# The memory stage of a two-layer decoder: one masking operation on a difference, the best one-hot by a relu on ScalarE, 1/Z on the one-hots, buffers of their own and a new order of work

## What is computed

```python
xn = (x - mu) * rsqrt(var + BN_EPS) * gamma + beta
q = (xn @ w_q.T).reshape(b, n, 2, h, kd).transpose(2, 0, 1, 3, 4)
sim = einsum('pbnhd,hkpd->pbnhk', q, keys)            # 2 sides, 8 heads, 32 keys
s, i = top_k(sim, 8)                                  # the 8 best keys of each side
all_scores = sx[..., :, None] + sy[..., None, :]      # 64 pairs a head
scores, pk = top_k(all_scores, 8)                     # the 8 best pairs
o = gelu(inputs . key_in[idx]) * softmax(scores)
return sum over heads and pairs of o * key_out[idx]   # 1024 experts of 128 features
```

## Time and profile before

| | |
|---|---|
| median of three runs | 2841.72 us |
| the profiled execution, its own time | 2846.45 us |
| its span, first to last instruction | 2844.7 us |
| TensorE busy | 2507.1 us (88%) |
| VectorE busy | 2333.9 us (82%) |
| ScalarE busy | 1834.5 us (64%) |
| GpSimd busy | 1016.5 us (36%) |
| memory stage | from about 648 to 1431 us of the span |
| granted TensorE clock, mean | 0.934 |

### The profile page before, as it was taken

One profiled execution on the slowest core, in us unless ns is written; L12 is line 12 of the kernel. 1 busy time (PEld: TensorE's weight loads), 2 busy tenths in 40 slices (PEclk: granted clock), 3 DMA queues, 4 the chain that ended last, 5 costly groups with the idle time before them and its releaser, 6 DMA issues.

```text
span 2844.7 us, 95835 instructions
## 1 busy us (share of the span) xinstructions
PE 2507.1 (88%) x35786; PEld 1949.9 (69%) x35786; DVE 2333.9 (82%) x6239; ACT 1834.5 (64%) x3307; POOL 1016.5 (36%) x1045
## 2 busy tenths in 40 slices
PE   2999982776888888888789999989979999999999
PEld 2666651555777777777756666656678888888887
DVE  6999989786799999999779999868867777777776
ACT  1777763454566666666456666658857777777776
POOL 0444430006799999999722332211121000000000
PEclk9999995885799999999899999979959999999999
DMA  5000000000000000000010000011101111111111
GB/s 169 1 0 0 0 15 0 1 0 2 2 0 0 0 0 0 0 0 0 1 60 0 0 0 0 1 34 44 41 16 48 50 56 52 56 54 50 56 52 49
DMA packets 56796, 64.67 MB, mean 23 GB/s; under 512 B 7696, under 2 KB 35088, under 8 KB 56592
## 3 DMA queue, kind: packets, MB, share of 16 engines
q1 hardware_dynamic: 56720, 63.65, 7.4%
HBM read 59.17 MB, written 4.46 MB: 22 GB/s over the span
## 4 chain that ended last, share of the span: by engine, by line
PE 81%; DVE 10%; issue 5%; DVEq 1%; ACT 1%; POOL 1%; DMA 0%; ACTq 0%; POOLq 0%; SPq 0%
PE ps L1073 9%; PE ps L894 8%; PE ps L1062 5%; PE ps L921 5%; PE ps L936 4%; PE ps L1087 4%; PE ps L1164 4%; PE ps L1166 4%; PE ps L1142 4%; PE ps L1165 4%; PE ps L1144 4%; PE ps L1143 4%; DVE work L1596 3%; PE ps L908 3%; PE ps L949 2%
## 5 line engine op out<-in xcount | busy, mean ns | idle before, releaser
L484 POOL TENSOR_TENSOR work<-work,consts_sb 128x1024 f32<-128x1024 f32 x128 | 243.6, 1903 | 563.1 <-ACT work L612 563.1
L1073 PEld LDWEIGHTS ps<-work 32*32 32x32 f32 x16384 | 244.2, 145 | 124.8 <-issue 123.0
L1073 PE MATMUL ps<-work 32*32 32x32 f32 x16384 | 250.1, 226 | 74.2 <-DVE work L1596 61.3
L732 ACT ACTIVATE ps<-work 128x128 f32<-128x128 f32 x512 | 154.6, 354 | 236.5 <-DVE work L1578 225.4
L894 PE MATMUL ps<-work 128*128 128x512 f32 x512 | 262.1, 614 | 4.3 <-issue 4.3
L1726 DVE TENSOR_TENSOR h_low<-consts_sb,h_up 128x1024 fp32r<-128x1024 f32 x128 | 158.4, 1237 | 110.9 <-ACT h_up L803 110.7
L1142 PE MATMUL ps<-a_low,w_up 128*128 128x512 f32 x512 | 202.7, 396 | 1.5 <-DVE a_low L1701 0.9
L1164 PE MATMUL ps<-h_low,d_up 128*128 128x512 f32 x512 | 199.6, 390 | 2.3 <-DVE h_low L1726 2.3
L1726 DVE TENSOR_TENSOR h_low<-small_w,h_up 128x1024 fp32r<-128x1024 f32 x128 | 158.8, 1241 | 51.6 <-ACT h_up L803 51.6
L1144 PE MATMUL ps<-a_up,w_low 128*128 128x512 f32 x512 | 199.9, 391 | 0.0
L1143 PE MATMUL ps<-a_up,w_up 128*128 128x512 f32 x512 | 199.8, 390 | 0.0
(11 more groups left out here) (260 smaller groups left out, 6703.5 us busy)
## 6 DMA issues: line engine op xcount, KB each, us to landing
gates_spread<-gate_rows SPq DMA_DIRECT2D x128, 256.0 KB, 3.1
ctxT_all<-in_ctxT SPq DMA_DIRECT2D x1, 4096.0 KB, 12.9
work<-in_ctx SPq DMA_DIRECT2D x64, 64.0 KB, 1.8
work<-in_ctxT SPq DMA_DIRECT2D x64, 64.0 KB, 1.8
out<-x_all SPq DMA_DIRECT2D x16, 256.0 KB, 3.5
big<-in_up SPq DMA_DIRECT2D x1, 2048.0 KB, 8.5
consts_sb<-in_consts SPq DMA_DIRECT2D x1, 936.0 KB
w<-in_key_inT SPq DMA_DIRECT2D x1, 512.0 KB, 3.6
```

The source lines that it names most:

```text
L1073: ins = pe.matmul(psW[rows, n // 16, :, n % 16], XT[rows, T.u, :, n], YT[rows, T.u, :, n], start=True, stop=True)
```

## The change

GpSimd no longer builds the one-hot of the best key by a subtraction and a comparison. It takes the least kept product less the four terms for all heads at once, into a buffer LESS (`below_least`), and VectorE's `chosen` becomes one instruction: is the difference at most zero, times the term. The best one-hot comes from ScalarE: relu(1 + 2^100 * difference). The factor 1/Z is put on the two one-hots (`scaled_one_hots`, ScalarE, eight instructions, from SBUF into the strided layout `sides`) in place of the four terms (into PSUM). The differences have a buffer of their own (DIFF), so that exp is one instruction of 640 elements; IN2 becomes one of three rows of a buffer `hots`; psSim and psM get PSUM banks of their own. The lists of segments are in a new order, with larger lags on ScalarE, TensorE and VectorE, and `add_memory` is split in two.

```diff
+        DIFF = carve(BEST + 2 * NS)
-        IN2 = carve(2 * NS).rearrange("p (s h k) -> p s h k", s=2, h=PH)
+        hots = carve(3 * 2 * NS).rearrange("p (r s h k) -> p s r h k", r=3, s=2, h=PH)
+        IN2 = hots[:, :, 2]
+        LESS = w8[:, 0:NEXP].rearrange("p (n h k) -> p n h k", n=4, h=PH)
+        one_hot_sides = sides.rearrange("p (k a r h) -> p a r h k", a=4, r=2, h=PH)[:, 0:4:3]
...
-        psM = bank(4, 0)
-        psSim = ps[:, 7, :]
+        psM = bank(3, 0)
+        psSim = ps[:, 2, :]
...
                 need(pool, hot_ready, T.before(1))
+                need(pool, scaled_ready, T.before(1))
                 pool.tensor_tensor(IN2, keys_of(u), second, ALU.subtract).then_inc(less_second, 1)
...
-            def ranks(T):
-                need(pool, sides_ready, T.before(1))
-                pool.tensor_tensor(one_hot[0], keys_of(u), best_of(u)[:, :, :, 0:1].to_broadcast([P, 2, PH, NKEY]), ALU.subtract)\
-                    .then_inc(less_top, 1)
-                pool.tensor_scalar(one_hot[0], one_hot[0], 0.0, None, ALU.is_ge).then_inc(top_ready, 1)
-                pool.tensor_tensor(one_hot[1], IN2, one_hot[0], ALU.subtract).then_inc(hot_ready, 1)
-            staggered(nc, pool, NT, [(0, candidates), (0, terms), (0, ranks)])
+            def second_one_hot(T):
+                pool.wait_ge(top_ready, T.now())
+                pool.tensor_tensor(IN2, IN2, hots[:, :, T.u], ALU.subtract).then_inc(hot_ready, 1)
+            def below_least(T):
+                pool.wait_ge(t8_ready, T.now())
+                pool.wait_ge(terms_ready, T.now())
+                need(pool, xy_ready, T.before(1))
+                least = T8[:, u, :, TOPK - 1:TOPK].unsqueeze(1).to_broadcast([P, 4, PH, NKEY])
+                pool.tensor_tensor(LESS, least, terms_of(u), ALU.subtract).then_inc(share_ready, 1)
+            staggered(nc, pool, NT, [(0, candidates), (0, terms), (0, second_one_hot), (0, below_least)])
...
+                act.activation(EX[:, T.u, 0:BEST + 2 * NS], DIFF[:, :], ACT.Exp).then_inc(ex_ready, 1)
+            def best_one_hot(T):
+                act.wait_ge(d_ready, T.now())
+                need(act, scaled_ready, T.before(2))
+                act.activation(hots[:, :, T.u], keys_diff, ACT.Relu, scale=FAR, bias=1.0).then_inc(top_ready, 1)
+            def scaled_one_hots(T):
+                act.wait_ge(hot_ready, T.now())
+                act.wait_ge(rz_ready, T.now())
+                need(act, sides_ready, T.before(1))
                 for h in range(PH):
-                    ins = act.activation(psSH[:, :, h, :], terms_of(u)[:, :, h, :], ACT.Copy, scale=RZ[:, u, h:h + 1])
+                    ins = act.activation(one_hot_sides[:, :, :, h, :], one_hots_of(u)[:, :, :, h, :], ACT.Copy, scale=RZ[:, u, h:h + 1])
...
-            staggered(nc, act, NT, [(0, normed), (1, shares), (0, key_exps), (1, hidden)])
+            staggered(nc, act, NT, [(0, normed), (1, key_exps), (2, scaled_one_hots), (1, best_one_hot), (2, hidden)])
...
-            staggered(nc, pe, NT, [(0, key_scores), (2, spread_heads), (1, hidden), (3, mixed), (2, turn_weights)])
+            staggered(nc, pe, NT, [(3, spread_heads), (4, mixed), (2, hidden), (3, turn_weights), (0, key_scores)])
...
-                for h in range(PH):
-                    ins = dve.scalar_tensor_tensor(out=chosen_terms[:, :, h, :], in0=terms_of(u)[:, :, h, :],
-                                                   scalar=T8[:, u, h, TOPK - 1:TOPK], in1=psSH[:, :, h, :],
-                                                   op0=ALU.is_ge, op1=ALU.mult)
+                dve.scalar_tensor_tensor(out=chosen_terms, in0=LESS.rearrange("p n h k -> p (n h) k"), scalar=0.0,
+                                         in1=terms_of(u).rearrange("p n h k -> p (n h) k"), op0=ALU.is_le, op1=ALU.mult)\
+                    .then_inc(xy_ready, 1)
...
-            staggered(nc, dve, NT, [(0, top_keys), (0, less_best), (1, chosen), (2, turn_back), (0, top_pairs), (3, add_memory),
-                                    (1, turn_sides), (0, pair_sums), (2, gated), (0, pair_shares)])
+            staggered(nc, dve, NT, [(0, top_keys), (0, less_best), (4, add_memory), (2, turn_back), (4, stats_with_memory), (1, chosen),
+                                    (0, top_pairs), (1, turn_sides), (0, pair_sums), (2, gated), (0, pair_shares)])
```

59 lines of the change are left out of this document (28 added, 31 removed).

## The result

The changed kernel takes 2853.15 us (median of 6 runs, 2848.39 to 2857.20) against 2840.84 us of the kernel before on the same chip (6 runs, 2837.49 to 2845.20). The ratio is 1.0038, with a 95% interval of 1.0026 to 1.0050: it is slower, by 0.4%. The forecast was 2824 us, 0.6% faster, with a range from 2792 to 2852. The profiled execution took 2852.48 us with a span of 2850.7, so the span grew by 6.0 us.

What follows compares the result with a forecast made beforehand. GpSimd was taken to set the pace now, and a circle of waits after the change; 53 tiles by 0.15 us is 8, plus 10 at the ends, 18 us less: 2824 us, range 2792 to 2852.

Steps and rivals of the forecast that it cites:

- chosen (12): Forecast's spread: VectorE's chosen, taken as 1.7 us, could lie between 1.2 and 2.25; 12 us more at the upper end.
- the lock's length (7): Forecast's spread: if GpSimd locks VectorE out for all of second_one_hot's 1.08 us, not 0.95, 7 us more in all.
- The tile: Memory stage loop: steps of 11.6 and 10.8 us, mean 11.2, 0.15 less than now, 8 us over 53 tiles.
- The ends: First and last tiles of the memory stage: add_memory's waits for TensorE leave their place ahead of turn_sides; 10 us gained.
- The load of the exp table ... 1.28 us, every other tile: ScalarE, before key_exps' exp: the load is exposed in the loop's first step and hidden in the second; 1.28 us.
- L1559 to be held until 0.95 after second_one_hot starts, in every tile, because both hang on one event: VectorE's first subtraction of less_best, behind the scaled copies, is locked out by GpSimd; first step 11.6 us.
- The same step for the second tile: Loop's second step: candidates held by chosen until 3.4, terms at 3.75, the same 0.95 us hold; 10.8 us.
- no change: Rival: TensorE's clock dips or queueing around chosen keep the tile at 11.3 us; 2842 us; chance 0.12.
- one of the prediction's own signs of being wrong: Prediction wrong if less_best's first subtraction is short, the copies take 3 us or more, or VectorE waits for TensorE again.
- The sizes: Instruction times taken from similar ones: second_one_hot 1.08 us and below_least 1.90 on GpSimd, chosen 1.7 on VectorE.
- Strided writes are slow on ScalarE: Rival: the eight scaled copies pay for strides, 0.86 us later; 2856 us with the lock, chance 0.16; without, 2818, 0.10.
- No lock: Rival: GpSimd and VectorE miss each other, a tile takes 10.65 us, 2795 us; chance 0.20 with strides hidden.

Runs made afterwards that it cites:

- Run 10: Changed kernel with TensorE's hidden product moved behind the next tile's key scores: 2820.86 us, ratio 0.9933 to the kernel before.
- run 2: Changed kernel with the two waits of key_exps swapped: 2852.85 us, ratio 1.0036 to the kernel before.
- run 1: Changed kernel with less_best's first subtraction reading the first eight scores in PSUM, so the wrong eight keys: 2814.01 us, ratio 0.9898 to the kernel before.
- run 11: Changed kernel with a one-element Exp, its result unread, ahead of key_exps' waits: 2792.27 us, ratio 0.9828 to the kernel before.
- run 8: Changed kernel with the best eight in PSUM and sides laid out so chosen and the scaled copies write side by side: 2851.23 us, ratio 1.0044.
- run 12: Changed kernel with the best eight in PSUM and a one-element Exp ahead of key_exps' waits: 2791.72 us, ratio 0.9818 to the kernel before.
- run 7: Changed kernel with the best eight written to PSUM and a copy of the sixteen tops in SBUF: 2821.36 us, ratio 0.9942 to the kernel before.
- run 5: Changed kernel with less_best's first subtraction reading stand-in scores in PSUM and chosen written side by side over LESS: 2793.03 us, ratio 0.9842.
- run 13: Kernel before the change with a one-element Exp ahead of key_exps' waits: 2841.41 us, ratio 0.9985 to the kernel before without it.
- run 3: Changed kernel with VectorE's add_memory and its statistics moved behind turn_sides, turn_back and chosen earlier: 2874.42 us, ratio 1.0101 to the kernel before.

## Why the prediction was wrong

By its own sum: 53 tiles at 0.15 us less, and 10 us at the ends. Its spread up to 2840 us was too narrow by its own terms: chosen (12), the lock's length (7) and no gain at the ends (10) make 2853. That this is the measured time is luck: the ends gained, and the greater part of the loss came from below_least, which is in none of the three. Measured on the spans:

- **The tile** (11.2 us predicted, 11.96 measured): 50 tiles cost 28.8 us more than before where about 8 less was forecast. This is the step that failed.
- **The ends** (10 us forecast): tile 13 comes 11.9 us sooner after the first than before, and the drain behind the last less_best is 36.0 us against 38.4. That is 14 us. VectorE's 23.5 us of waiting for mixed in the first tiles are gone, and 11.9 us for spread_heads (L1616) stand in their place, so mechanism and sign were right.
- **Not in the sum:** everything behind the memory stage takes 8 us less (last section). 28.8 - 14 - 8 is about the 6.0 us of the span, with 0.3 for the stage's start.

Within the tile:

- **"The load of the exp table ... 1.28 us, every other tile": right as a mechanism, wrong as a price.** It was added as 1.28 in the first step's chain. The runs price it at 1.2 us a tile in the mean (11.96 against 10.78), nearly twice what half of 1.28 would be: 1.2 in the first step, as added, and 1.2 more in the mean of the second, where it had none, since it decides whether the subtraction meets below_least.
- **"L1559 to be held until 0.95 after second_one_hot starts, in every tile, because both hang on one event": held in the first step, but too short a hold, and for another reason.** VectorE doesn't hang on the copies there either. `turn_sides` (L1609) follows `top_pairs` (L1584), which waits for candidates that chosen held up, and starts 0.16 to 0.89 us behind the copies' end; L1574 comes 0.1 us behind L544's start in 15 of the 25 first steps and 0.6 to 0.8 in 10. It doesn't matter, since GpSimd does hang on the copies and L1574 is let go at L544's end wherever it came in. Above, L1574 effectively began 0.29 before its end, 1037.86, 1.15 us after L544's start: the hold lasts nearly all of the instruction. So it did in the first pair of the earlier trace rows: L535 ends at 674.78 and L1559 at 674.93, 0.15 behind it. The 0.95 belongs to L535's 1.09 us; the prediction took it for a constant, because L1559 beside L539 gave nearly the same. With the copies ending 0.14 later and L529 0.06 later than my terms, 11.6 becomes 11.97. The Trainium skill (SBUF — State Buffer, "SBUF: two separate sides") has the lock held for the whole instruction. Here the two-input subtractions agree with it (ends 0.15 and 0.16 us after L553's and L544's); it would have given 0.13 of the 0.37 missing.
- **The same step for the second tile: wrong, and this is the failure.** In the second step turn_sides starts 1.15 us behind the scaled copies' end, and VectorE's way from the last less_best goes through chosen, top_pairs, turn_sides and gated; it arrives 1.0 to 1.8 us behind second_one_hot's start, and the instruction it meets is below_least, of 2.0 us, which the change itself puts there. I had costed below_least for GpSimd's own time only and never asked whom it locks out. 16 steps of 12.64 and 9 of 10.72 make 11.95 in place of 10.8. With 11.97 in the first, that is all of the mean. L1574's mean of 1.19 us is the 1.2 that was forecast, by luck: in the second step it is a mixture of 0.3 to 0.5 and 1.6 to 2.1.
- **TensorE's turn_weights in front of gated:** the rival "no change" named dips of the clock, and I held against it that the waits had moved behind independent work. A slow mixed makes gated up to 0.8 us late, and between 0.24 and 0.31 us of lateness the step goes from 10.7 to 12.6. Run 10 removes the wait and all long steps with it. So VectorE does wait for TensorE again, one of the prediction's own signs of being wrong. The granted clock is 0.86 without long steps too (run 2), 0.92 with the load late and nothing held on the subtraction (run 1), and 0.95 with the load ahead (run 11); what lowers it isn't shown.
- **The sizes:** second_one_hot 1.29 us for 1.08 (neither input is broadcast, where L518's second is), below_least 2.02 for 1.90, chosen 1.95 for 1.7. Chosen's cost lay not on VectorE but on GpSimd, whose L514 and L517 stand still beside it, 0.6 and 0.8 us a tile in the mean. The prediction let it delay the second step's candidates only.
- **"Strided writes are slow on ScalarE"** was rightly put below the forecast: the eight copies take 2.56 us at a stride, 2.43 side by side (run 8). Each one does pay the price of L712, 0.49 us for 0.39, but they start 0.29 us apart either way, as the prediction had argued. The time that I gave this rival, 2856 us, is near the measured one by luck, for another reason.
- **"No lock", 2795 us:** that rival's 10.65 us a tile is what run 12 gives (10.72), but it takes the load ahead as well; with the subtraction's lock gone alone it is 11.24 to 11.35 us (runs 1 and 7), and 10.93 with a shorter chosen besides (run 5).

## What to carry to other kernels

A circle of waits through two engines that lock each other out has no fixed price for a delay: 1.3 us of a table load in every other tile became 2.4 us for the pair here. So when GpSimd gets a new long instruction with SBUF inputs, ask which two-input VectorE instruction can meet it in each step of the loop, and lay the steps of the loop out apart, since a mean hides a step that is 2 us off. Two cheap cures are worth trying first: one input in PSUM (1.0% here), and a one-element activation that draws the table load ahead of the wait (2.1% here; the two together gave no more). The second works only where nothing long stands ahead of it on ScalarE (run 13).

## What the hardware showed that I had not expected

- **The lock goes both ways and passes between instructions.** chosen on VectorE holds GpSimd's L517 from 0.36 to 1.95 us, and a held VectorE instruction gets in between two back-to-back GpSimd ones (run 11: L1576 ends at 1011.69, 0.15 behind L545's end, with L554 starting at 1011.48 already). Nor is every hold as long as the instruction: beside GpSimd's L539, a TENSOR_SCALAR of 2.46 us, VectorE's L1559 ends 1.24 to 1.34 us after its start in all 42 tiles of the kernel before in which it is held (from 800 to 1390 us).
- **Where a table load stands is not where the code says.** With the two waits swapped it waited behind less_best in both steps (run 2); a one-element Exp put it ahead in both, and in the kernel before, behind eight copies, moved nothing (run 13).
- **A stride** costs 0.75 us on 1024 elements: at 256 bytes for VectorE's write (1.95 against 1.20), at 128 bytes for each transposing read (1.99 against 1.23). ScalarE's writes of 128 elements at 256 bytes take 0.49 us against 0.39, but eight of them in a row end only 0.13 us later. The Trainium skill charges each crossing of a 16-byte line (SBUF — State Buffer, "Door 1: The DMA port swizzle"); each of these instructions agrees, and the row of eight hides it.
- **The clock far behind the edit.** At the change of stages some 440 us after the memory stage TensorE's granted clock is half for 20 us longer in the kernel before. The windows 440 to 460 us behind each stage's end, of the kernel before:

```profile
1870.50:1890.50 20.00, 20.00 (x201) 12.98 (x203) 9.76 (x23) 9.51 (x12) 2.09 (x7) 0.51 0.10 27
```

and, of the changed one, the window 440 to 460 us behind its own:

```profile
1884.70:1904.70 20.00, 19.93 (x354) 14.15 (x346) 16.57 (x40) 16.49 (x22) 3.69 (x13) 1.00 0.16 45
```

In the 20 us ahead of these windows the clock was 0.50 and 0.57. The rest of the program behind the memory stage is 1414.5 us before and 1406.4 after. It was 1406 to 1410 in most of the variants, 1414 in runs 12 and 13 and 1418 in runs 3 and 8, so it isn't tied to one edit; what decides it stays open.
